# A cross-attention decoder on one core: waits for values of another turn moved from the end of the loop to their readers, loads issued ahead of the store, a new order of steps

## The reference

```
# layer 0: 16 heads of 64
q = rms(x) @ wq;  k = ctx @ wk;  v = ctx @ wv
x = x + softmax(q k^T) v @ wo
# layer 1: 16 heads of 16
x = x + MHA(ln1(x), ln1(x), causal) @ m_proj_w + m_proj_b
x = x + MHA(ln2(x), ctx)            @ c_proj_w + c_proj_b
x = x + relu(ln3(x) @ f_w1 + f_b1) @ f_w2 + f_b2      # 256 -> 1024 -> 256
```

## Time and profile before

| what | value |
|---|---|
| median of 3 runs | 5888.48 us (5873.54 to 5890.43) |
| the profiled execution: time, span | 5875.75 us, 5874.0 us |
| TensorE (PE) busy | 5309.4 us, 90% of the span |
| ScalarE (ACT) busy | 4329.6 us, 74% |
| VectorE (DVE) busy | 2190.4 us, 37% |
| mean granted TensorE clock | 0.952 |
| DMA over the span | mean 13 GB/s |

### The profile page before, as it was taken

One profiled execution on the slowest core, in us unless ns is written; L12 is line 12 of the kernel. 1 busy time (PEld: TensorE's weight loads), 2 busy tenths in 40 slices (PEclk: granted clock), 3 DMA queues, 4 the chain that ended last, 5 costly groups with the idle time before them and its releaser, 6 DMA issues. The chain is left out here.

```text
span 5874.0 us, 137598 instructions
## 1 busy us (share of the span) xinstructions
PE 5309.4 (90%) x48328; PEld 4185.2 (71%) x48328; DVE 2190.4 (37%) x5823; ACT 4329.6 (74%) x17665; POOL 530.7 (9%) x845
## 2 busy tenths in 40 slices
PE   6989999999999899999999998999899999999997
PEld 5767777677777677777777777777677777777775
DVE  3334333333333343333333333433333334334332
ACT  3777777787777777777877777778778777777785
POOL 0001001000000010010000000100100001001000
PEclk9999999999999999999999999999999999999998
DMA  2000000000000000000000000000000000000000
GB/s 69 10 12 10 14 11 11 14 8 14 14 8 14 12 10 14 10 12 14 8 14 14 8 14 12 10 14 8 14 14 8 14 12 10 14 12 10 14 8 8
DMA packets 64805, 76.10 MB, mean 13 GB/s; under 512 B 4592, under 2 KB 62768, under 8 KB 63920
## 3 DMA queue, kind: packets, MB, share of 16 engines
q1 hardware_dynamic: 63920, 64.19, 3.5%
HBM read 47.40 MB, written 16.78 MB: 11 GB/s over the span
## 5 line engine op out<-in xcount | busy, mean ns | idle before, releaser
L452 ACT ACTIVATE ps<-ps,negmax 128x77 f32<-128x77 f32 (+2 forms) x6144 | 2070.5, 377 | 255.4 <-DVE negmax L664 255.4
L452 ACT ACTIVATION_READ_ACCUMULATOR ps<-ps,negmax 128x1 f32 x6144 | 1542.6, 255 | 0.0
L664 DVE TENSOR_REDUCE negmax<-ps 128x4 f32<-128x308 f32 (+2 forms) x1792 | 929.5, 563 | 699.5 <-PE ps L891 349.7
L405 POOL TENSOR_TENSOR small<-small 128x1 f32<-128x1 f32 (+1 forms) x448 | 263.5, 588 | 5148.7 <-DVE small L638 2674.8
L659 DVE TENSOR_TENSOR zTl<-ps,zTh 128x256 fp32r<-128x256 f32 x512 | 210.6, 422 | 1241.4 <-ACT zTh L432 1241.4
L838 PE MATMUL ps<-wf,coT 128*128 128x256 f32 x2048 | 475.7, 385 | 10.9 <-issue 7.8
L838 PE MATMUL ps<-wo,coT 128*128 128x256 f32 x2048 | 469.4, 382 | 0.2 <-issue 0.2
L517 ACT ACTIVATE probs<-ps 77x512 f32<-77x512 f32 x512 | 275.5, 588 | 229.2 <-PE ps L943 226.2
L838 PEld LDWEIGHTS ps<-wf,coT 128*128 128x128 f32 x2048 | 379.8, 190 | 90.6 <-issue 43.8
L525 ACT ACTIVATE probs<-ps 128x512 f32<-128x512 f32 x768 | 388.2, 617 | 63.7 <-PE ps L982 63.7
L838 PEld LDWEIGHTS ps<-wo,coT 128*128 128x128 f32 x2048 | 379.2, 190 | 56.9 <-ACT ps L452 10.0
(11 more groups left out here) (181 smaller groups left out, 11816.6 us busy)
## 6 DMA issues: line engine op xcount, KB each, us to landing
xin<-x_dram SPq DMA_DIRECT2D x64, 256.0 KB, 3.4
x<-x_dram SPq DMA_DIRECT2D x64, 256.0 KB, 2.7
out<-xr SPq DMA_DIRECT2D x64, 256.0 KB, 4.0
cin<-ctx_dram SPq DMA_DIRECT2D x64, 77.0 KB
wk<-wk_dram SPq DMA_DIRECT2D x1, 1024.0 KB, 5.3
wo<-wo_dram SPq DMA_DIRECT2D x1, 1024.0 KB, 8.1
wf<-f_dram SPq DMA_DIRECT2D x1, 1024.0 KB, 10.6
probs<-wq_dram SPq DMA_DIRECT2D x1, 1024.0 KB, 9.9
```

The costliest lines, as they stand in the source:

```text
L405: nc.gpsimd.tensor_tensor(rstd[:, stage, ts], veps[:, stage, ts], minus_half[:, ts], ALU.pow).then_inc(rstd_ready[stage], 1)
L452: ins = nc.scalar.activation(scores, scores, ACT.Exp, bias=negmax[w][:, t, h:h + 1], accum_out=sums[w][:, t, h:h + 1])
L664: nc.vector.tensor_reduce(dst, bank(s)[:, 0:heads * width].rearrange("p (h k) -> p h k", h=heads), AX_X, ALU.max, negate=True).then_inc(ma ...
```

## The change

Six things, in the code's order. (1) A new order of the 84 steps. `skA.1-` and `f2.1` still end the turn, and `mt.0-`, `rms+`, `pv.1.1` still begin it. `qsA-` now stands ahead of `qsB.0-` and `qsB.1-`, and `qsB.1-` directly ahead of `ln.1-` and the four `h`; `v0.1+ v0.0+ k0.1+` stand earlier. `sk0.3-` replaces `sk0.2-` behind `pv.1.1`, then both `proj.1`. (2) `landed` looks the reader's sources up itself, also in the turn before (`Counts.source`, `past`): what comes from another turn is waited for in front of its reader. (3) The wait for CARRIED at the end of each turn is gone from the loop. It stays (`settle`) at the end of the straight code ahead of the loop. ScalarE's `ln` step gets the same treatment. (4) All bank counters begin at FIRST = 24 in place of 0: VectorE and TensorE each add 24 to eight counters once, in front of everything. (5) SyncE's loop now asks for the residual x1 of this turn, then for the next tokens `xin`, then for the next context `cin`, and only then stores y. (6) No product, exponential or transfer is added or taken away.

```diff
 LOOP_ORDER_TEXT = """
-    mt.0- rms+ pv.1.1 sk0.2- proj.1.0 stat.2.0 proj.1.1 stat.2.1 norm.2.0 norm.0+ sk0.1- sk0.3- sk0.0-
-    norm.2.1 turn.2.0 turn.0+ turn.2.1 pv0.3- pv0.2- pv0.1- q1.2 pv0.0- qs2.1 q0.3+ wo.0- qs2.0 stat.1.0-
-    wo.1- norm.1.0- stat.1.1- ln.2 norm.1.1- q0.1+ q0.0+ q0.2+ mt.2 turn.1.0- turn.1.1- sk2.0 sk2.1 q1.1-
-    k1- pv.2.0 pv.2.1 qsB.1- cv- proj.2.1 proj.2.0 stat.3.0 ck- stat.3.1 norm.3.0 ctx+ v1- qsB.0-
-    norm.3.1 turn.3.0 k0.0+ k0.1+ turn.3.1 v0.1+ qsA- ln.1- h.0 h.3 h.2 h.1 v0.0+ qs0.1.2+ qs0.1.3+ mt.1-
-    qs0.1.0+ qs0.1.1+ f2.0 skB- skA.0- qs0.0.3+ qs0.0.1+ qs0.0.0+ qs0.0.2+ pv.1.0- ln.0+ skA.1- f2.1
+    mt.0- rms+ pv.1.1 sk0.3- proj.1.1 proj.1.0 sk0.1- sk0.2- sk0.0- stat.2.0 stat.2.1 norm.0+ norm.2.0
+    norm.2.1 turn.0+ turn.2.0 turn.2.1 pv0.2- pv0.1- pv0.0- pv0.3- q1.2 q0.3+ qs2.1 wo.0- qs2.0 stat.1.0-
+    norm.1.0- wo.1- stat.1.1- ln.2 norm.1.1- q0.1+ q0.2+ q0.0+ mt.2 turn.1.1- turn.1.0- sk2.1 sk2.0 q1.1-
+    k1- pv.2.0 pv.2.1 cv- ck- ctx+ qsA- proj.2.1 proj.2.0 v1- v0.1+ stat.3.0 v0.0+ k0.1+ stat.3.1
+    norm.3.0 norm.3.1 turn.3.0 turn.3.1 qsB.0- k0.0+ qsB.1- ln.1- h.0 h.3 h.1 h.2 qs0.0.3+ qs0.1.3+ mt.1-
+    qs0.0.0+ qs0.1.0+ f2.0 skA.0- skB- qs0.1.1+ qs0.0.1+ qs0.1.2+ qs0.0.2+ pv.1.0- ln.0+ skA.1- f2.1
 """
...
+    def all(self, order):
+        for step in order:
+            self.next(step)
+        return self
+
+    def source(self, step, reader):
+
+        if STAGES[step] == STAGES[reader]:
+            return self.of.get(step)
+        return self.past.of.get(step) if self.past else None
+
...
         def orders(eng, run):
 
-            for order, before, uses, count, batch in turns:
+            past = None
+            for k, (order, before, uses, count, batch) in enumerate(turns):
                 if batch is not None:
-                    run(order, Counts(before, None, 0), batch)
+                    past = Counts(before, None, 0, past, turns[min(k + 1, len(turns) - 1)][4] is None)
+                    run(order, past, batch)
                 else:
                     with eng.Fori(0, NB - 2) as i:
-                        run(order, Counts(before, uses, i), (i + 1, i, i + 2))
+                        earlier = {r: [a - b for a, b in zip(before[r], uses[r])] for r in RINGS}
+                        run(order, Counts(before, uses, i, Counts(earlier, uses, i).all(order)), (i + 1, i, i + 2))
+                    last = {r: [a + (count - 1) * b for a, b in zip(before[r], uses[r])] for r in RINGS}
+                    past = Counts(last, None, 0).all(order)
 
         def probs_slot(step, r):
...
-            with sp.Fori(2, NB) as b:
-
-                sp.wait_ge(c_used, b)
-                sp.dma_start(cin[0:S, :], ctx[bass.ds(b, 1)].rearrange("a s c -> (a s) c")).then_inc(c_in, 16)
-                sp.wait_ge(x_used, b)
-                sp.dma_start(xin[:], x_v[bass.ds(b, 1)].rearrange("a p t c -> (a p) t c")).then_inc(x_in, 16)
+            sp.wait_ge(c_used, 2)
+            sp.dma_start(cin[0:S, :], ctx[2]).then_inc(c_in, 16)
+            sp.wait_ge(x_used, 2)
+            sp.dma_start(xin[:], x_v[2]).then_inc(x_in, 16)
+            with sp.Fori(2, NB - 1) as b:
 
                 sp.wait_ge(x1_used, b - 1)
                 sp.dma_start(x1[:], x_v[bass.ds(b - 1, 1)].rearrange("a p t c -> (a p) t c")).then_inc(xres_in, 16)
+                sp.wait_ge(x_used, b + 1)
+                sp.dma_start(xin[:], x_v[bass.ds(b + 1, 1)].rearrange("a p t c -> (a p) t c")).then_inc(x_in, 16)
+                sp.wait_ge(c_used, b + 1)
+                sp.dma_start(cin[0:S, :], ctx[bass.ds(b + 1, 1)].rearrange("a s c -> (a s) c")).then_inc(c_in, 16)
 
                 sp.wait_ge(y_ready, b * 2 - 2)
                 sp.dma_start(out_v[bass.ds(b - 2, 1)].rearrange("a p t c -> (a p) t c"), y[:]).then_inc(y_stored, 16)
+            sp.wait_ge(x1_used, NB - 2)
+            sp.dma_start(x1[:], x_v[NB - 2]).then_inc(xres_in, 16)
+            sp.wait_ge(y_ready, NB * 2 - 4)
+            sp.dma_start(out_v[NB - 3], y[:]).then_inc(y_stored, 16)
             sp.wait_ge(x1_used, NB - 1)
...
+            for bank_free in free:
+                dve.sem_inc(bank_free, FIRST)
...
+            for bank_full in full:
+                pe.sem_inc(bank_full, FIRST)
...
-            def landed(c, u, *steps):
-
-
+            def landed(c, u, reader):
 
                 last = {}
-                for step in sorted((st for st in steps if st in c.of), key=lambda st: c.of[st]["place"]):
-                    for s, v, _ in c.of[step]["bank"]:
+                found = [(st, c.source(st, reader)) for st in sources(reader)]
+                for st, taken in sorted((x for x in found if x[1]), key=lambda x: (STAGES[x[0]] == STAGES[reader], x[1]["place"])):
+                    for s, v, _ in taken["bank"]:
                         last[s] = v
                 for s, v in last.items():
                     if s not in [x[0] for x in u["bank"][:1]]:
...
-                landed(c, {"bank": []}, *CARRIED)
+                if c.settle:
+                    for step, reader in CARRIED:
+                        if step in c.of:
+                            for s, v, _ in c.of[step]["bank"]:
+                                pe.wait_ge(free[s], v)
```

More of the change, by code:

```diff
@@ L22 @@
 RINGS = {"bank": 8, "split": 1, "chain": 1, "max": 1}
+FIRST = 24
 USES = {
@@ L108 @@
                 if step[0] in SUMMED[k] and (STAGES[step] + 1) % 3 < (STAGES["ln", k] + 1) % 3]
-CARRIED = [p for step in LOOP_ORDER for p in sources(step) if (STAGES[p] + 1) % 3 < (STAGES[step] + 1) % 3]
+CARRIED = [(p, step) for step in LOOP_ORDER for p in sources(step) if (STAGES[p] + 1) % 3 < (STAGES[step] + 1) % 3]
 def slot_uses(order):
@@ L120, with __init__ @@
 class Counts:
-    def __init__(self, before, per_turn, turn):
+    def __init__(self, before, per_turn, turn, past=None, settle=False):
         self.before, self.per_turn, self.turn = before, per_turn, turn
+        self.past, self.settle = past, settle
         self.at = {r: 0 for r in RINGS}
@@ L172, in decoder @@
              (part(0, 1), 1, (NB - 1, NB - 2, None)), (part(1), 1, (None, NB - 1, None))]
-    before = {r: [0] * n for r, n in RINGS.items()}
+    before = {r: [FIRST if r == "bank" else 0] * n for r, n in RINGS.items()}
     turns = []
@@ L454, in exponential_sums, with summed @@
                 ins.then_inc(free[s], 1)
-            def summed(c, scores):
-                last = {s: v for st in scores for s, v, _ in c.of[st]["bank"]}
+            def summed(c, reader):
+                taken = [c.source(st, reader) for st in LOOP_ORDER if st[0] in SUMMED[reader[1]]]
+                last = {}
+                for of in taken:
+                    for s, v, _ in of["bank"] if of else ():
+                        last[s] = v
                 for s, v in last.items():
@@ L508, in run @@
                         w = int(step[1] > 0)
-                        summed(c, [st for st in c.of if st[0] in SUMMED[step[1]]])
+                        summed(c, step)
                         nc.scalar.activation(logs[w][:], sums[w][:], ACT.Ln).then_inc(logged[step[1]], 1)
@@ L545, in run @@
                         ins.then_inc(free[s], 1)
-                summed(c, [st for st in c.of if st in CARRIED_SUMS])
+                if c.settle:
+                    for st in CARRIED_SUMS:
+                        if st in c.of:
+                            for s, v, _ in c.of[st]["bank"]:
+                                act.wait_ge(free[s], v)
             act.wait_ge(consts_ready, 1)
@@ L864, in run @@
                     elif n == "q0":
-                        landed(c, u, *sources(step))
+                        landed(c, u, step)
                         columns_product(u, "wq0", 2 * step[1], xTh, xTl)
                     elif n in ("k0", "ck"):
-                        landed(c, u, *sources(step))
+                        landed(c, u, step)
                         s = take_bank(u)
```

7 lines of the change are left out of this document (4 added, 3 removed).

## The result

| kernel | median, us | runs |
|---|---|---|
| before | 5889.45 | 4 (5873.54 to 5894.07) |
| changed | 5338.37 | 4 (5334.42 to 5343.11) |

The ratio is 0.9069, with a 95% interval of 0.9050 to 0.9088. The time lies inside the range, beside its lower edge, and on the first rival's 5337 us rather than on the forecast's 5550. The 212 us between forecast and result aren't noise: the four runs lie within 9 us. The profiled execution took 5337.84 us. Since this document takes small steps apart, most of what follows is told in **turns**: the distance between two branches of TensorE's loop. 61 x 8.77 = 535 us, of 538 between the profiled executions.

A forecast was written before the change was run, and what follows sets the result against it. TensorE's stream, busy 90%, was taken to bound the kernel, with two code-wait holes a turn. 7.5 - 1.2 (clock) - 1.0 (order) = 5.3 us a turn, 323 us over 61 branches: 5550 us; own range 5450 to 5650, stated range 5330 to 5700.

The forecast's parts named there:

- first rival: No second hole: longer code moves the block boundary past the loop's head, saving 3.5 us a turn more; 5337 us, chance 0.15.
- Wait at the turn's end: Without it TensorE branches at about 2937.1 instead of 2941.4, before `f2.1` ends; the first hole goes; gain 7.5 us a turn.
- I estimate about ten: TensorE's code ahead of the loop grows about ten instructions, moving the block boundary to about the first product of `pv.1.1`.
- Fetch at 3.4 us: TensorE's branch at the turn's end still fetches code, taking 3.99 - 0.6 = 3.4 us, done before `f2.1` ends.
- second hole 2.3: TensorE idles some 2.3 us after `mt.0`, at about the first product of `pv.1.1`, waiting for the second code block.
- half of the turns at the low clock: After the 2.3 us idle, the clock falls in half of the turns: -1.2 us a turn, ends 0 and -3.8.
- Loads "no gain of its own": Moving `xin` and `cin` ahead of the store starts VectorE's statistics about 4.4 us earlier; only cover for the 7.5 us gain.
- New waits, 0: Some 15 waits in front of readers, 1.2 us of TensorE's sequencer a turn; cost 0, at most 1.2 us.
- New order, -1.0: `qsB.1` ahead of `ln.1` and `h` stalls TensorE 1.2 us before `f2.0`; term -1.0 us a turn, ends +0.8 and -2.5.
- The clock that falls in every turn: Rival: at the turn's head the clock falls every turn and stays low as long as now; 5711 us, chance 0.12.
- A branch that doesn't overlap: Rival: TensorE's branch waits for the array to drain, gaining only 0.6 us; 5875 to 5830 us, chance 0.06.
- Slower by ScalarE: Rival: ScalarE's exponentials and `h` pile up before `f2.0`, stalling TensorE 7.5 us; 6105 us, chance 0.04.

The follow-up runs named there:

- b_pad24: The kernel before with 24 increments of an unused semaphore in TensorE's code ahead of the loop, nothing else; 5628.37 us, ratio 0.9562.
- b_newsp_r: The kernel before, its loop held by 24 increments as in b_pad24, with the changed kernel's SyncE loop (loads ahead of the store); 5385.54 us, ratio 0.9141.
- a_oldorder: The changed kernel with the step order of before, loop still held; 5317.85 us, ratio 0.9032.
- a_oldsp: The changed kernel with SyncE's loop as before, context and tokens asked for behind the store; 5660.17 us, ratio 0.9610.
- a_pad233: The changed kernel with 233 semaphore increments ahead of the loop, putting its head where it lay within a block before; 5630.85 us, ratio 0.9559.
- a_endwait_f: The changed kernel with TensorE's wait for all carried banks back at each turn's end and 240 increments ahead of the loop, code fetched; 5943.87 us, ratio 1.0112.
- a_endwait_r: The changed kernel with TensorE's wait for all carried banks back at each turn's end and 7 increments ahead of the loop, code held; 5408.11 us, ratio 0.9187.
- a_pad160: The changed kernel with 160 semaphore increments ahead of the loop, which then touches 7 blocks; 5357.43 us, one run.
- a_pad200: The changed kernel with 200 semaphore increments ahead of the loop, which then touches 8 blocks; 5460.21 us, one run.

## Why the prediction came out as it did

Where the 8.77 us of a turn went, by steps between kernels, all with held code behind the first. Each is one thing, but "waits at their readers" holds parts 2 to 4 of the change together:

| step | from, to | turn, us | us |
|---|---|---|---|
| code held | before, b_pad24 | 89.87 to 85.83 | -4.04 |
| loads ahead of the store | b_pad24, b_newsp_r | to 81.87 | -3.96 |
| waits at their readers | b_newsp_r, a_oldorder | to 80.71 | -1.16 |
| new order | a_oldorder, changed | to 81.10 | +0.39 |

The shares depend on the path: the waits are worth 5.07 us with fetched code, the loads 5.24 behind early waits (a_oldsp), holding the code 4.23 in the changed kernel (a_pad233) and 8.21 where the wait stands at the end (a_endwait_f against a_endwait_r).

**Wait at the turn's end: right.** The branch 3.6 us ahead of `f2.1`'s end stood in the changed kernel and in a_pad233.

**"I estimate about ten": the step that failed.** The text let the block boundary move to the first product of `pv.1.1` and leave a hole of 2.3 us. The shift was 23 and took the boundary past the head. With the count right, the forecast would have been the first rival, which had 0.15. It went through on its condition, but its picture was too small as well: it spoke of a first block that reaches far into the turn. What happened is that no block was fetched at all. That it met the time to 1 us is luck: it was priced at 3.5 us a turn where 4.23 was measured, and the forecast beneath it at 5.3 where a_pad233 gained 4.54, and the two errors cancel. That the result lies in the stated range is luck for the forecast's mechanism too: the range was drawn down to 5330 to hold this rival's time, and the forecast's own began at 5450.

**The rule of the Trainium skill: set aside too soon, and read in part.** The row showed a fetch in every turn, and I let the row refute the rule. The rule (the Trainium skill, Runtime: NRT & Kernel Launch, Instruction fetch mechanics) has two halves: 2048 instructions for TensorE, in blocks of 256, and a stall for a taken branch "whose target isn't in the current 2-page window". I used the first and left the window out. Neither half alone fits the rows. By the window the changed kernel's branch should stall, since its target lies 1609 instructions back; it took 0.21 us with no packet fetched. By the 2048 the kernel before should stay; it was fetched. The rows say: 1609 instructions over 7 blocks stay, over 8 they don't, though 8 x 256 is 2048 (a_pad160 and a_pad200). That section of the Trainium skill names no such reserve; a block asked for beyond the loop's end would be one, 7 + 1 = 8, but that is the reading above and not shown.

**Fetch at 3.4 us, second hole 2.3, half of the turns at the low clock:** where the code is fetched (a_pad233), the median was 3.57, the hole of the turn looked at 1.91 with 0.54 of clock behind it. The turn came to 85.33 in place of 84.57, and the increments took another 36 us, which is why a_pad233 stood at 5631 and not at 5550. The mechanism was right there. The clock's term is a little short: by the trace's record of the granted clock it was low in 52 of the 61 turns and not in half of them, 3.02 us a turn on average; half of that, 1.5 us, is my estimate of the cost, against 1.2. The mean granted clock of the execution says about the same: 0.976 against 0.993 in the changed kernel. The other 0.46 us of the miss stay open, and more than that, since the second hole (1.91 against 2.3) and the new order (below) came out cheaper than their terms.

One of the two rows that the clock's term rested on was read short. The idle stretch of 1.75 us ended where the clock fell, not where TensorE went on; that was at 5777.59, after 2.44 us:

```profile
5777.59 0.66 PE L811 MATMUL ps<-ident,z 128*128 128x128 f32 x2 [2.44 <-DVE z L650]
```

So the rows of before set 2.44 us, behind which the clock was low, against 2.30, behind which it wasn't.

**Loads "no gain of its own": half right.** They were named as the cover of the first term. But the cover was worth 4 to 5 us a turn, the largest single lever beside the code, and what it costs if it is gone was not worked out. It was there to be read: 2946.13 for the statistics, with `proj.1.0` behind them in VectorE's queue.

**New waits, 0: right, as far as can be told.** a_oldorder has them all and is 1.16 us a turn faster than b_newsp_r, which has the one at the end in their place; that one alone costs 1.09 (a_endwait_r), so nothing is left for the others.

**New order, -1.0:** the sign was right, the size was 0.39. The stall at `f2.0` was 0.70 us and not 1.2.

**The other rivals.** The clock that falls in every turn: the windows of the changed kernel show 1.00. A branch that doesn't overlap: refuted by a_pad233, where 3.57 us of it stand beside `f2.1`. Its price was not worked out rightly either: 0.6 us gained against 1.0 lost is 5900 us, and 5830 to 5875 leaves the 1.0 out. Slower by ScalarE: not seen; the wait at `f2.0` is 0.70 us. What can undo the gain is another mechanism: with the end wait kept and code fetched (a_endwait_f) a turn is 90.40 us, 0.53 longer than before.

## What to carry to other kernels

A loop whose code nearly fills an engine's instruction memory can have a time that depends on its address, here by 4 to 8 us of a turn of 80 to 90: before believing that an edit made the gain, count the packets of the instruction queue in both profiles, and shift the loop by a few idle instructions as a control. Put no wait right ahead of a loop's branch: the same one cost 1.1 us with code held and 5.1 with code fetched. When two stalls stand side by side, price each as if the other were gone: here the second, a load queued behind a store, was as long as the first.

## What was not expected of the hardware

- TensorE held a loop of 1609 instructions over 7 blocks (19 to 20 packets in the whole program, branch 0.21 us). Over 8 blocks it fetched 9 packets a turn (branch 3.6 to 3.9 us) at heads 235, 236 and 246 instructions behind a boundary, and in 32 of 61 turns at 202.
- The ninth packet of a turn was begun ahead of the branch, by 5.2 us (before) and 1.2 us (a_pad233). In a_pad200 a branch was slow exactly where such a packet fell together with it.
- TensorE ran out of code at one place of its program, whatever the shift: instruction 1473 or 1474, and 1729 or 1730, which is 256 further.
- An increment of a semaphore by TensorE's sequencer cost 0.14 to 0.16 us: 21.8 us for 160, 36.3 us for 233.
- The granted clock fell to 0.54 behind a hole of 1.91 us (a_pad233) and to 0.57 behind one of 2.65 us (b_pad24), where it had held over 2.30 us in one place of before. Holes of the same kind and nearly the same length did both: of a_pad233's, 1.63 to 2.30 us long, 52 in 61 were followed by a low clock; over a_pad200's loop with its 31 holes of 1.12 to 1.96 us the mean is 1.00.
